# Second norm and expert gate, taken apart by batch: batch 0 beside the last attention half, the others between the first expert tiles

## The reference

```python
logits = normalize(x2) @ normalize(sim_matrix) - sigmoid(gates)      # 16 per token
gated = relu(logits); mask = gated > 0                               # or the best two, if none is active
rw = softmax(where(mask, gated, -inf))
q, k, v = (sum over e of rw[e] * (x2 @ proj[e]) for each of the three)   # 64 wide
attn = causal_softmax(q @ k.T / 8) @ v                               # within one batch
out = sum over e of (attn * rw[e]) @ o_proj[e]
```

## Time and profile before

| what | value |
| --- | --- |
| median of 3 runs | 1410.54 us (1410.22 to 1411.25) |
| the profiled execution's own time | 1409.21 us |
| its span in the profile | 1407.0 us |
| DVE busy | 1182.9 us, 84% |
| PE busy | 1223.9 us, 87% |
| ACT busy | 1103.2 us, 78% |
| POOL busy | 1026.6 us, 73% |
| mean granted clock of TensorE | 0.972 |

### The profile page before, as it was taken

One profiled execution on the slowest core, in us unless ns is written; L12 is line 12 of the kernel. 1 busy time (PEld: TensorE's weight loads), 2 busy tenths in 40 slices (PEclk: granted clock), 3 DMA queues, 4 the chain that ended last, 5 costly groups with the idle time before them and its releaser, 6 DMA issues. The chain is left out here.

```text
span 1407.0 us, 24022 instructions
## 1 busy us (share of the span) xinstructions
PE 1223.9 (87%) x8370; PEld 750.4 (53%) x8370; DVE 1182.9 (84%) x1937; ACT 1103.2 (78%) x2031; POOL 1026.6 (73%) x714
## 2 busy tenths in 40 slices
PE   2789999999999999999999999988851599999997
PEld 1344444445444444444444454444431598988897
DVE  5899999999999999999999999999856376767665
ACT  2899999999999999999999999999733355656553
POOL 2788898899898899989889989989924444434330
PEclk9999999999999999999999999999975799999999
DMA  4232111121211112111111211110031776768570
GB/s 111 71 89 63 51 31 51 31 62 44 57 52 31 52 34 65 42 53 52 31 52 38 64 40 51 31 31 1 1 58 25 128 127 123 133 110 144 101 130 10
DMA packets 184598, 86.85 MB, mean 62 GB/s; under 512 B 150176, under 2 KB 166048, under 8 KB 184480
## 3 DMA queue, kind: packets, MB, share of 16 engines
q1 hardware_dynamic: 184480, 85.33, 28.6%
HBM read 7.68 MB, written 2.10 MB: 7 GB/s over the span
## 5 line engine op out<-in xcount | busy, mean ns | idle before, releaser
L1246 DVE TENSOR_REDUCE negmax<-score_ps 128x1 f32<-128x1024 f32 x512 | 618.3, 1218 | 47.1 <-PE score_ps L609 45.1
L490 POOL TENSOR_TENSOR prob<-prob 128x1024 f32<-128x1024 f32 x256 | 604.1, 2360 | 50.0 <-ACT prob L966 34.0
L925 ACT ACTIVATE prob<-score_ps,negmax 128x1024 f32<-128x1024 f32 x512 | 571.6, 1119 | 60.5 <-DVE negmax L1246 59.7
L609 PE MATMUL score_ps<-ka,qa 128*128 128x512 f16 x1024 | 307.8, 382 | 82.8 <-ACT prob L925 72.5
L638 PE MATMUL attn_ps<-probT,v_sb 128*64 128x512 f32 x1024 | 276.2, 619 | 0.8 <-ACT attn_nT L973 0.8
L632 PE MATMUL trans_ps<-ident,prob 128*128 128x128 f32 x2048 | 269.1, 274 | 0.8 <-POOL prob L490 0.4
L632 PEld LDWEIGHTS trans_ps<-ident,prob 128*128 128x128 f32 x2048 | 238.4, 141 | 55.9 <-issue 2.0
L557 POOL TENSOR_TENSOR xs<-xnT,rw_all 128x2048 f32<-128x2048 f32 x32 | 115.5, 3611 | 168.6 <-DVE prob L1379 161.9
L488 POOL TENSOR_SCALAR prob<-prob,ccol 128x1024 f32<-128x1024 f32 x192 | 216.1, 1125 | 2.6 <-DVE ccol L1259 2.6
L609 PEld LDWEIGHTS score_ps<-ka,qa 128*128 128x128 f16 x1024 | 80.5, 97 | 217.9 <-ACT prob L925 152.4
L332 DVE COPY probT<-trans_ps 128x512 f32<-128x512 f32 x256 | 174.4, 681 | 1.8 <-PE trans_ps L632 1.8
(11 more groups left out here) (195 smaller groups left out, 1324.6 us busy)
## 6 DMA issues: line engine op xcount, KB each, us to landing
qa<-split SPq DMA_DIRECT2D x256, 64.0 KB, 2.0
ka<-split SPq DMA_DIRECT2D x256, 64.0 KB, 2.0
xg<-xnT SPq DMA_DIRECT2D x16, 512.0 KB, 3.0
resid<-in_L_attn_x SPq DMA_DIRECT2D x4, 512.0 KB, 6.0
wg<-in_L_attn_Wkv SPq DMA_DIRECT2D x32, 64.0 KB, 2.0
out<-prob SPq DMA_DIRECT2D x32, 64.0 KB, 2.5
wg<-in_L_attn_Wq SPq DMA_DIRECT2D x16, 64.0 KB, 1.9
xsT<-prob SPq DMA_TRANSPOSE x64, 4.5
```

Of the source, the lines that this page charges most:

```text
L490: pool.tensor_tensor(prob1[:, n % PROBS, :], prob1[:, n % PROBS, :], prob2[:, n % 4, :], ALU.add).then_inc(mix_ok, 1)
L609: mm = pe.matmul(score_ps[:, sub, kh * HALF:(kh + 1) * HALF], qa[:, par, head * 2 + sub, q0:q0 + P], ka[:, par, head * 2 + sub, kh * HALF: ...
L925: act.activation(prob2[:, n % 4, :] if sub else prob1[:, n % PROBS, :], score_ps[:, sub, :], ACT.Exp, bias=negmax[:, s % 2, sub:sub + 1], ...
L1246: dve.tensor_reduce(negmax[:, s % 2, sub:sub + 1], score_ps[:, sub, :], AX.X, ALU.max, negate=True).then_inc(max_ok, 1)
```

## The change

The norm of the second block and its gate are no longer made for all batches together.

- In the last iteration DVE makes the mean of batches 0, 1 and 2 in slots 3, 11 and 19, and POOL centres batches 0 and 1 after the first and the third unit of the last half, into `x2n` in place. The last unit's mix is scaled on ACT and added on DVE. The trailing slots end 4 slots after the last unit; what is left of the last two halves is written out by hand, mixed with norm and gate of batch 0, which now work on 8 token tiles at a time.
- The rest of norm and gate for batches 1 to 3 is cut into pieces that are called from the loop over the expert tiles: on DVE `extra` just behind the low part and `extra_end` at the end of a tile, on ACT `extra` at the end of a tile, on PE `between` behind expert groups 1 and 3, on POOL between the first `xs`.
- The buffers are laid out anew so that the weights fit where q and k inputs lay; their DMAs start when the last q and k have been stacked. The split of the weights is made in parts (experts 0 to 7, 8 to 11, 12 to 15, then the output weights), and the expert groups of tile 0 wait for the parts one by one.
- The last half's output copies go to another buffer, the gate's PSUM banks are shared with those of the tiles, and new waits (`g_V`, `g_seen`) keep these apart.

The diff, cut to its core:

```diff
-EARLY = 3
-POOL_BATCHES = (0, 1)
-LN2_SLOT = SLOTS + 1
+SUM_SLOTS = {3: 0, 11: 1, 19: 2}
+LAST_SLOTS = SLOTS + TRANS_LAG
+LAST_UNIT = STEPS * UNITS - 1
+HALVES = 2 * STEPS
...
+        W_PARTS = ((0, 8), (8, 12), (12, 16))
...
-            sp.wait_ge(resid_ok, 2 * STEPS)
+            sp.wait_ge(filled["v1"], STEPS)
+            for kind in "qk":
+                sp.wait_ge(stacked[kind], 256 * (STEPS - 1) + 128)
             for n, w in enumerate((eq, ek, ev)):
                 sp.dma_start(ew[:, :, n * DE:(n + 1) * DE], w.rearrange("e c d -> c e d")).then_inc(experts_in, 16)
...
                 for u in range(8):
-                    mix(8 * h + u, (8 * h + u) % PROBS)
+                    if 8 * h + u < LAST_UNIT:
+                        mix(8 * h + u, (8 * h + u) % PROBS)
+                    if h == HALVES - 1 and u in (0, 2):
+                        centre(u // 2)
...
+            def scale_by_experts(m):
+                if m % NT == 0:
+                    pool.wait_ge(g_n, m // NT + 1)
+                    pool.wait_ge(rw_ok, m // NT + 1)
+                if m:
+                    pool.wait_ge(xs_lo, m)
...
+            scale(0)
+            pool.wait_ge(g_nrm, 1)
+            weights_low(0)
+            root(HALVES - 2)
+            norm(HALVES - 2)
+            weights_low(1)
+            scale_by_experts(0)
+            weights_low(2)
+            root(HALVES - 1)
+            scale_by_experts(1)
+            pool.wait_ge(cols_ok, HALVES - 1)
+            norm(HALVES - 1)
+            scale(1)
+            centre(2)
+            scale_by_experts(2)
+            pool.wait_ge(w_hi, 4)
+            pool.tensor_tensor(eow_split[:, 1, :, :], eow[:, :, :], eow_split[:, 0, :, :], ALU.subtract).then_inc(w_lo, 1)
+            centre(3)
+            scale_by_experts(3)
+            scale(2)
+            scale_by_experts(4)
+            scale(3)
+            for m in range(5, B * NT):
+                scale_by_experts(m)
```

On PE:

```diff
+            def between(m, group):
+                if m == 0 and group == 1:
+                    pe.wait_ge(resid_ok, HALVES - 1)
+                    columns(HALVES - 1)
+                elif m == 0 and group == 3:
+                    project(HALVES - 1)
+                    gate_transposes(1)
+                elif m == 1 and group == 3:
+                    pe.wait_ge(resid_ok, HALVES)
+                    gate_logits(1)
+                    gate_transposes(2)
+                elif m == 2 and group == 3:
+                    gate_logits(2)
+                    pe.wait_ge(g_seen, 2)
+                    gate_transposes(3)
+                elif m == 3 and group == 3:
+                    gate_logits(3)
```

On ACT, called at the end of a tile:

```diff
+            def extra(m):
+                if m == 0:
+                    gate_high(1)
+                    seed(2, g_var, 0)
+                elif m == 1:
+                    seed(2, g_nrm, 2)
+                    gate_high(2)
+                    ln2_squares(3)
+                elif m == 2:
+                    seed(3, g_nrm, 2)
+                    gate_high(3)
+                elif m in (3, 6, 9):
+                    gate_exp(m // 3)
```

On DVE, where `extra` is called behind the low part of tile m + 2 and `extra_end` at the end of the tile:

```diff
+            def ln2_mean(b):
+                dve.wait_ge(resid_ok, 2 * G * (b + 1))
+                dve.tensor_reduce(per_tile(0, b), rows(resid, b), AX.X, ALU.add).then_inc(g_sum, 1)
+                dve.wait_ge(g_sum, b + 1)
+                dve.tensor_scalar(per_tile(1, b), per_tile(0, b), -1.0 / C, None, ALU.mult).then_inc(g_mean, 1)
+            def ln2_root(b):
+                dve.wait_ge(g_var, b + 1)
+                dve.wait_ge(g_y, 4 * b + 2)
+                polished(per_tile(4, b), per_tile(2, b), per_tile(5, b), per_tile(0, b), g_v, g_scale)
+            def norm_squares(b):
+                link(dve.tensor_tensor(per_tile(5, b), per_tile(0, b), per_tile(0, b), ALU.mult), g_v)
+                link(dve.tensor_tensor(per_tile(5, b), per_tile(5, b), per_tile(7, b), ALU.mult), g_v)
+                link(dve.tensor_scalar(per_tile(2, b), per_tile(5, b), RSQ_SHIFT, RSQ_LEAST, ALU.mult, ALU.max), g_nrm)
+            def norm_root(b):
+                dve.wait_ge(g_y, 4 * b + 4)
+                polished(per_tile(4, b), per_tile(2, b), per_tile(5, b), per_tile(3, b), g_v)
+                link(dve.tensor_scalar(per_tile(3, b), per_tile(3, b), RSQ_SHIFT ** 0.5, 1.0 / GATE_LEAST, ALU.mult, ALU.min), g_v)
...
+            ln2_variance(1)
+            norm_squares(0)
+            gate_low(0)
+            norm_root(0)
+            last_stat(HALVES - 2)
+            gate_read(0)
+            gate_top(0)
+            last_root(HALVES - 2)
+            gate_chosen(0)
+            gate_weights(0)
+            last_add(HALVES - 2)
+            last_stat(HALVES - 1)
+            x_low(0, 0)
+            ln2_root(1)
+            norm_squares(1)
+            last_root(HALVES - 1)
+            x_low(1, 1)
+            norm_root(1)
+
+            def extra(m):
+                if m == 0:
+                    last_add(HALVES - 1)
+                    ln2_mean(3)
+                    ln2_variance(2)
+                elif m == 1:
+                    ln2_root(2)
+                    norm_squares(2)
+                elif m == 2:
+                    gate_read(1)
+                    norm_root(2)
+                    ln2_root(3)
+                    norm_squares(3)
+                elif m in (3, 6, 9):
+                    gate_chosen(m // 3)
+                elif m in (4, 7, 10):
+                    gate_weights(m // 3)
+                if m == 3:
+                    norm_root(3)
+                    gate_low(3)
+                elif m == 4:
+                    gate_read(3)
+
+            def extra_end(m):
+                if m == 0:
+                    gate_low(1)
+                elif m == 1:
+                    ln2_variance(3)
+                    gate_low(2)
+                elif m in (2, 5, 8):
+                    if m == 2:
+                        gate_read(2)
+                    gate_top((m + 1) // 3)
```

More of the change, by code:

```diff
@@ L526, in _ @@
                 units(h, True)
[L528 to L546, removed]
-                pool.wait_ge(w_hi, n + 1)
[L548 to L555, removed]
+            def weights_low(n):
+                e0, e1 = W_PARTS[n]
+                pool.wait_ge(w_hi, n + 1)
+                pool.tensor_tensor(ew_split[:, 1, e0:e1, :], ew[:, e0:e1, :], ew_split[:, 0, e0:e1, :], ALU.subtract).then_inc(w_lo, 1)
@@ L794, in tiles2 @@
                         pe.wait_ge(mT_lo, 2 * (m - 3))
-                        if not (first and t == 4):
+                        if m == 4:
+                            pe.wait_ge(w_lo, 4)
+                        else:
                             pe.wait_ge(y_done, m - 4)
@@ L1112, in polished @@
                 link(dve.tensor_scalar(t, t, -0.5, 1.5, ALU.mult, ALU.add), sm)
-                link(dve.tensor_tensor(u, t, y, ALU.mult), sm)
+                link(dve.tensor_tensor(u, t, y, ALU.mult), done or sm)
             dve.wait_ge(const2_in, 16 * 2)
@@ L1358, in _ @@
-            assert links[g_v.name] == GEXP, links
-            dve.tensor_scalar(gs[:, 0, :], best, 0.0, float(E), ALU.is_gt, ALU.mult).then_inc(g_top, 1)
-            dve.wait_ge(g_top, 2 * NTB + 1)
-            link(dve.tensor_copy(top2f[:, :, :], top8i[:, :, 0:2]), g_v)
-            link(dve.tensor_tensor(top2f[:, :, :], top2f[:, :, :], gs[:, 0, :].unsqueeze(2).to_broadcast([P, NTB, 2]), ALU.add), g_v)
-            for n in range(2):
-                dve.tensor_tensor(gl[:, 2 + n, :, :], per_expert(iota[:, :]),
-                                  top2f[:, :, n:n + 1].to_broadcast([P, NTB, E]), ALU.is_equal).then_inc(g_top, 1)
@@ new lines, in gate_top @@
+            def gate_top(b):
+                lg = rows(gl[:, 0, :, :], b)
+                link(dve.tensor_tensor(lg, rows(gl[:, 1, :, :], b), per_expert(sgate[:, :]), ALU.subtract), g_v)
+                for t in range(b * NT, (b + 1) * NT):
+                    dve.max(out=top8[:, t, :], in_=gl[:, 0, t, :]).then_inc(g_top, 1)
+                dve.wait_ge(g_top, TOPS * b + NT)
+                for t in range(b * NT, (b + 1) * NT):
+                    dve.max_index(out=top8i[:, t, :], in_max=top8[:, t, :], in_values=gl[:, 0, t, :]).then_inc(g_top, 1)
@@ new lines, in gate_weights @@
+            def gate_weights(b):
+                dve.wait_ge(g_exp, b + 1)
+                link(dve.tensor_tensor(rows(gl[:, 1, :, :], b), rows(gl[:, 6, :, :], b), rows(gl[:, 5, :, :], b), ALU.mult), g_v)
+                link(dve.tensor_reduce(per_tile(0, b), rows(gl[:, 1, :, :], b), AX.X, ALU.add), g_v)
+                link(dve.reciprocal(per_tile(1, b), per_tile(0, b)), g_v)
+                link(dve.tensor_tensor(rows(rw_all, b), rows(gl[:, 1, :, :], b), per_token(per_tile(1, b)), ALU.mult), rw_ok)
```

409 lines of the change are left out of this document (238 added, 171 removed).

## The result

The changed kernel takes 1442.24 us (median of 4 runs, 1440.01 to 1443.0) against 1410.74 us of the kernel before: a ratio of 1.0224, 95% interval 1.0212 to 1.0236. It is slower by 31.5 us; 1436 had been forecast, with 1399 to 1448 as the range. The profiled run took 1440.01 us with a span of 1438.2, 31.2 above the span before.

What follows compares the result with a forecast made beforehand. The prediction took DVE, ACT, POOL and PE as all nearly full in the last attention iteration, and PE as the bound from tile 5. Its terms, -0.8 + 22.0 + 4.0 = +25.2 us, gave 1436 us, range 1399 to 1448.

Steps and rivals of the forecast that it cites:

- First expert tile: Start of the expert phase: first expert matmul at 1052.9 instead of 1092.54, a gain of 39.6 us.
- M: End of unit 254's mix on POOL in the last attention iteration, forecast at 1019.6 us; later times count from it.
- Rival 3: Attention half pays full price and last halves queue on DVE; tile 0 only 28 us earlier, 1447 us, chance 0.10.
- The hold: Small DVE operations with data in SBUF wait until POOL's xs is over; cost between nothing and 3.61 us, 3.61 taken.
- Rival 1: xs does not hold the small DVE operations, or pieces fall where POOL waits; 1396 us, faster, chance 0.22.
- rival 2: Holds of about half the length, or half of the pieces meeting POOL; 1403 to 1423 us, chance 0.13.
- The four rows: Profile evidence before the change: four operations out of four that met a POOL instruction were held; none beside xs.
- Tile starts up to tile 5: Expert tiles 0 to 5: held pieces use up the lead; tile 5 at 1138.6 against 1139.40, 0.8 us left.
- the tile's own 4.0: Tile 4, from the end of gate_weights(1) at M+115.0 to the start of tile 5 at M+119.0: 4.0 us.
- Tiles 5 to 10: Gate pieces between low half and copy to p2T count in full: 22.0 us lost, plus 4.0 for the clock.
- The clock: PE's lower granted clock after stops in four of tiles 5 to 10: 1.0 us each, 4.0 (bounds 0 and 10).
- Sum: Whole kernel: -0.8 + 22.0 + 4.0 = +25.2 us, profiled span 1407.0 to 1432.2, time 1436.

Runs made afterwards that it cites:

- lead_alone: Changed kernel with norm and gate of batches 1 to 3 left out on all engines, batch 0's weights copied: 1372.45 us.
- the probe: Kernel before, with two unused 128x8 tensor_tensors added on DVE right behind the low half in twelve tiles (14 to 25): 1482.39 us.
- probe_one: Kernel before, with two unused 128x8 reciprocals added on DVE right behind the low half in twelve tiles: 1416.53 us.

## Why the prediction was right

**First expert tile.** M was put at 1019.6 and is 1019.9; the first xs at 1040.3 and is 1041.2; the first expert matmul at 1052.9 and is at 1054.65. The 39.6 us are 37.9. One term was too small, the tensor_scalar behind each of the three sums, which was held for 1.25 us and not 0.77; M was not later for it. Rival 3 (28 us) is out, and lead_alone shows that the lead is kept to the end if nothing follows.

**The hold.** This step decided the sign, and no row of before showed it beside xs: 3.61 was taken, the upper of its two bounds. Measured are 3.54 to 3.72 where an operation starts with xs, 3598 ns in the probe. Rival 1, no hold (1396), and rival 2, half of it (1403 to 1423), are out. The four rows had been enough, though one was read loosely: L1356 ended at 1073.70, 0.56 us behind the weight split (1073.14), the other three within 0.04 us of POOL. The rule of the Trainium skill (SBUF — State Buffer, Who interferes with whom), that a Vector instruction with two SBUF inputs and a GpSimd instruction that reads SBUF lock each other out and that a reduction on this chip never contends, agrees with this trace: L1529 took 3.72 us beside xs, and the reduction L1547 ran beside xs in 0.28 us. The tensor_scalar L1395, with one input in SBUF, was held as well (3.54); which mode it ran in no run shows. That a reciprocal passes (203 ns) is shown by probe_one.

The prediction's own wording was too wide: not every such operation waits. Its sum for gate_weights (0.3 + 3.6 + 0.3) has the second link held; in the trace the second and the third link passed and the fourth took 3.04. The total is nearly the same, 3.9, since the chain ends behind xs whichever link meets it.

**Tile starts up to tile 5**, forecast (1019.6 and the term of the text) and measured:

| tile | 0 | 1 | 2 | 3 | 4 | 5 |
| --- | --- | --- | --- | --- | --- | --- |
| forecast | 1052.9 | 1074.9 | 1091.6 | 1109.6 | 1126.2 | 1138.6 |
| measured | 1054.65 | 1073.74 | 1089.48 | 1108.86 | 1126.10 | 1141.29 |

Five of them lie within 2.2 us. Part of that is luck, for two errors cancel: the held pieces ended earlier than forecast (norm_squares(3) at 1103.53 and not 1107.2), and what follows them in a tile took longer (5.3 us to the start of tile 3 where 2.4 had been allowed). In tile 4 only the second error is left, and tile 5 is 2.7 late. gate_weights ended at 1134.40 as forecast (1134.6); the term that was too small is "the tile's own 4.0", which took 6.9 (1134.40 to 1141.29). It was sized from DVE alone, but PE had stood 4.34 us for DVE's count, and its next 24 matmuls took 3.44 us where 2.14 is usual.

**Tiles 5 to 10.** 26.0 forecast, 29.1 measured. The four pieces were right: gate_chosen 5.9 forecast, 5.7 measured in tiles 6 and 9 (in tile 6 from 1155.33 to 1161.05), gate_weights 4.2 forecast, 3.9 measured in tiles 7 and 10. gate_top was put at 0.9 each in tiles 5 and 8 and costs 0.3 (tile 5 takes 8.60 us, before 8.31) and nothing (tile 8 takes 10.14, as before): it stands behind lo2, where the idle time is a reserve. The clock was mis-sized: 1.0 per stop, 4.0 in all, where PE's busy time shows 7.7. The windows above divide the 29.1 without a rest: 21.4 idle time of PE, for which the prediction has 22.0, and 7.7 clock, for which it has 4.0. The pieces on DVE make 19.3 of the 21.4 (twice 5.7 and 3.9) and gate_top 0.3; 1.8 us are not assigned to a piece.

**Sum.** +25.2 forecast, +31.2 measured in the span: 2.7 at tile 5, 3.1 in tiles 5 to 10, 0.2 behind them. The error is what a stop costs beyond its own length, mostly the clock; the mechanism held.

Not tried: the weights' DMAs put back to their old place, which the prediction priced at a wait of up to 25 us on POOL.

## What to carry to other kernels

A short DVE operation with its data in SBUF, of the forms that were held here, costs as much as the POOL instruction that it meets, so place it by POOL's timetable: here a move of four lines to the end of the tile gave back 31.5 us. Before work is put "in between" in a loop that PE bounds, ask of each place what is queued behind it: behind the low half everything counted in full, with a loss of clock on top of the longer stops; with gate_chosen and gate_weights behind lo2 tiles 5 to 10 took 4.9 us more than before and not 29.1. A counter that another engine waits for is such a place too, even when it stands for no data (tiles 2, 3, 4 and 10). A lead that is won at the start of a phase is only worth what the phase lets stand, and leaving the rest out (lead_alone) says in one run how much that could be.

## What the runs showed of the hardware

- The hold is shown in the duration of the held instruction, not as idle time, and it works both ways. POOL's centring of batch 2 (1056.86) met a running low half (1056.00 to 1059.04) and took 3939 ns instead of 1900; that low half itself had begun beside POOL's scaling (to 1056.90) and took 3.04 us instead of 2.29:

```profile
L533 POOL TENSOR_TENSOR xnT<-resid,gs x4: 1894/1900/3939, 994.9 to 1071.3; 128x1024 f32<-128x1024 f32 x4
...
L1553 DVE TENSOR_TENSOR prob<-xs,prob x32: 2272/2292/3042, 1046.8 to 1390.5; 128x2048 f16<-128x2048 f32 x32
```

- It depends on the form and not on the size: beside an xs of 3.61 us a tensor_tensor of 128x8 took 3598 ns and a reciprocal of 128x8 203.
- A stop of PE of some us cost more than its length: 3.8 us of added DVE work in front of the copy cost 6.0 us a tile, with a granted clock of 0.83 where it had been 1.00, while 0.43 us cost 0.55 at an unchanged clock of 1.00.
